# Narrow key and digit loads issued by ScalarE, three in eight high one-hots by ScalarE, and a re-paced copy of x in a graph kernel

## What is computed

```
h = x @ Wn.T + bn;  e = edge_attr @ We.T + be
a = softmax over edges of one dst of leaky_relu(sum((h[src] + e) * attn))
x = layernorm(x + relu(segment_sum(h[src] * a, dst)))
mean = segment_sum(x[dst], src) / max(count, 1)
out = layernorm(x + x @ W1.T + b1 + mean @ W2.T + b2)
```

## Time and profile before

| What | us |
|---|---|
| median of 3 runs (1452.16 to 1456.42) | 1452.87 |
| profiled execution, its own time | 1450.54 |
| its span, first to last instruction | 1448.8 |

### The profile page before, as it was taken

How to read it: one execution, slowest core, us unless ns; L and a number is a source line. 1 busy time by engine, 2 the same in 40 slices (tenths; PEclk the granted TensorE clock), 3 DMA queues, 4 the chain that set the end, 5 groups by cost and what they waited for, 6 DMA issues and landing times.

```text
span 1448.8 us, 26746 instructions
## 1 busy us (share of the span) xinstructions
PE 1247.1 (86%) x7210; PEld 1052.6 (73%) x7210; DVE 1088.4 (75%) x3970; ACT 784.8 (54%) x1768; POOL 749.9 (52%) x731
## 2 busy tenths in 40 slices
PE   4687837992299999589999999999998999999994
PEld 3576726882188888478888888888886888877783
DVE  8588947889655555188888888988888787867761
ACT  5744582560044444257777777777774444544542
POOL 1067763777767777634334103555530555655563
PEclk9999978996599999889999999999999999999997
DMA  6399865998556666556666767898872233223221
GB/s 189 119 277 293 261 180 191 296 313 299 198 82 97 91 100 87 77 187 219 218 226 216 231 216 260 294 298 296 301 243 85 91 98 92 88 90 94 86 79 42
DMA packets 118161, 260.71 MB, mean 180 GB/s; under 512 B 23505, under 2 KB 56872, under 8 KB 118084
## 3 DMA queue, kind: packets, MB, share of 16 engines
q1 hardware_dynamic: 75738, 193.82, 40.9%
q0 software_dynamic: 40128, 64.45, 19.7%
q10 hardware_dynamic: 2218, 1.58, 0.3%
HBM read 182.23 MB, written 130.49 MB: 216 GB/s over the span
## 4 chain that ended last, share of the span: by engine, by line
PE 63%; DMA 10%; POOL 7%; issue 7%; ACT 6%; DVE 5%; SPq 1%; POOLq 0%; ACTq 0%; DVEq 0%
PE bank L1248 35%; PE bank L1238 9%; PE bank L1293 5%; PE bank L1289 5%; PE bank L1245 4%; PE bank L1228 4%; DMA xin<-z_scratch,idx_src 3%; DMA yout<-low_digits_scratch 3%; POOL out_rows L467 3%; ACT aggn L604 3%; POOL xin L464 2%; DMA X<-in_x,idx_src 2%; PE bank L1177 2%; DMA order_scratch<-pay,rank_i 1%; ACT X L609 1%
## 5 line engine op out<-in xcount | busy, mean ns | idle before, releaser
L1248 PE MATMUL bank<-w1T,xT 128*128 128x256 f32 x1968 | 491.4, 380 | 0.0
L1248 PEld LDWEIGHTS bank<-w1T,xT 128*128 128x128 f32 x1968 | 343.7, 191 | 66.5 <-issue 0.3
L473 POOL DMA_INDIRECT order_scratch<-pay,rank_i x200 | 195.0, 975 | 233.6 <-DVE xin L749 106.5
L566 ACT ACTIVATE yout<-bank,nmr,rstd 128x256 f32<-128x256 f32 x492 | 251.7, 577 | 8.1 <-DVE nmr L752 8.0
L557 ACT COPY xT<-bank 128x512 f32<-128x512 f32 x346 | 203.0, 588 | 37.6 <-PE bank L1238 29.0
L916 DVE BATCH_NORM_STATS2 stats<-bank 128x6 f32<-128x512 f32 x246 | 168.5, 694 | 60.7 <-PE bank L1248 60.3
L916 DVE BATCH_NORM_STATS2 stats<-xin 128x6 f32<-128x512 f32 x246 | 158.3, 685 | 73.8 <-DMA xin<-z_scratch,idx_src 52.2
L665 ACT COPY agg<-bank 128x257 f32<-128x257 f32 (+1 forms) x200 | 74.3, 372 | 221.9 <-PE bank L1293 215.1
L512 POOL DMA_INDIRECT z_scratch<-xin,idx_out x100 | 156.4, 1564 | 56.9 <-ACT xin L678 33.8
L749 DVE TENSOR_SCALAR xin<-xin,stats,rstd 128x256 f32<-128x256 f32 x492 | 171.8, 411 | 1.0
L467 POOL DMA_INDIRECT out_rows<-yout,idx_out x100 | 100.0, 1000 | 139.6 <-DMA xin<-z_scratch,idx_src 67.8
(11 more groups left out here) (187 smaller groups left out, 1915.6 us busy)
## 6 DMA issues: line engine op xcount, KB each, us to landing
z_scratch<-in_x SPq DMA_DIRECT2D x125, 400.0 KB
xin<-z_scratch SPq DMA_DIRECT2D x97, 512.0 KB, 4.4
out_rows<-yout SPq DMA_DIRECT2D x97, 512.0 KB, 3.1
yout<-keys_scratch SPq DMA_DIRECT2D x50, 256.0 KB, 6.7
kB<-sorted_scratch SPq DMA_DIRECT2D x50, 256.0 KB, 3.3
yout<-low_digits_scratch SPq DMA_DIRECT2D x50, 128.0 KB, 8.0
xin<-in_edge_attr SPq DMA_DIRECT2D x12, 512.0 KB, 8.8
order_scratch<-pay,rank_i POOLq DMA_INDIRECT x200
```

Source lines behind the costliest of these rows:

```text
L473: g.indirect_dma_start(out=order_dram[k], out_offset=bass.IndirectOffsetOnAxis(ap=rank_i[k][:, t:t + 1], axis=0), in_=pay[:, t, :], in_off ...
L566: a.activation(yout[hu][0:rows, j, :], bank_of(j // 2)[0:rows, (j % 2) * D:(j % 2 + 1) * D], ACT.Identity, bias=nmr[0:rows, slot, j:j + 1] ...
L1248: ins = mm(to, buf[:, jj, c, 0:n], w[:, c, :], start=False, stop=i == len(terms) - 1 and c == 1)
```

## The change

The key scratch becomes 16-bit unsigned and the low-digit scratch 8-bit, so a key spread is 128 KB instead of 256 and a low-digit spread 64 KB instead of 128. VectorE makes the 16-bit copy by one more instruction per sort, ahead of the float copy. The spreads go from SyncE's queue to ScalarE's: three before the DST loop, in the middle of the DST histogram, then the pair of quad n+3 after the odd table copy of quad n. ScalarE makes the high one-hots of tiles 3, 7 and 1 of each eight, VectorE the other five. SyncE sends 20 copies of x beside the DST one-hots, then waits at quad n for VectorE to have used the keys of n quads, and sends one copy at even and two at odd DST quads. The block of 24 copies in the SRC part is unchanged in the text, but stands behind these waits.

```diff
-    keyrow_dram = [nc.dram_tensor(f"keys_scratch{k}", [T, P], F32).ap() for k in (DST, SRC)]
-    lowrow_dram = [nc.dram_tensor(f"low_digits_scratch{k}", [T, P], BF16).ap() for k in (DST, SRC)]
+    keyrow_dram = [nc.dram_tensor(f"keys_scratch{k}", [T, P], U16).ap() for k in (DST, SRC)]
+    lowrow_dram = [nc.dram_tensor(f"low_digits_scratch{k}", [T, P], U8).ap() for k in (DST, SRC)]
...
+        def high_by_act(t):
+            return t % GT == 3 or t % (2 * GT) == 1
...
+            for i in range(10):
+                sp.wait_ge(s_onehot, 2 * i + 1)
+                copy_x(2)
 
             for k in (DST, SRC):
-                sp.wait_ge(s_keyd[k], 32)
                 for q in range(Q):
-                    n = k * Q + q
-                    wait(sp, s_lbT, n - 3)
-                    wait(sp, s_lbA, n - 3)
-                    sp.dma_start(lowB[n % 4], spread(lowrow_dram[k], q)).then_inc(s_lb[n % 4], 16)
-                    wait(sp, s_kbu, n - 3)
-                    sp.dma_start(keyB[n % 4], spread(keyrow_dram[k], q)).then_inc(s_kb[n % 4], 16)
+                    wait(sp, s_kbu, k * Q + q)
                     if k == DST and q % 2 == 1 and q >= 5:
                         load_features((q + 3) // 2)
-                    copy_x(2 if k == DST else 1 if q >= 4 else 0)
+                    copy_x(1 + q % 2 if k == DST else 1 if q >= 4 else 0)
                     if k == SRC and q == 3:
                         for i in range(Q // 2):
                             sp.wait_ge(s_onehot, Q + 2 * i + 1)
                             copy_x(2)
...
-                at = [(GT * q + j, gap_hi[2 * (n % 2) + j // 2]) for j in (1, 3)]
+                at = [(GT * q + j, gap_hi[2 * (n % 2) + j // 2]) for j in range(GT) if high_by_act(GT * q + j)]
...
+            def load_spreads(n):
+                if n >= 2 * Q:
+                    return
+                k, q = n // Q, n % Q
+                if q == 0:
+                    act.wait_ge(s_keyd[k], 32)
+                wait(act, s_lbT, n - 3)
+                wait(act, s_lbA, n - 3)
+                act.dma_start(lowB[n % 4], spread(lowrow_dram[k], q)).then_inc(s_lb[n % 4], 16)
+                wait(act, s_kbu, n - 3)
+                act.dma_start(keyB[n % 4], spread(keyrow_dram[k], q)).then_inc(s_kb[n % 4], 16)
...
+                    if k == DST and q == Q // 2:
+                        for n in range(3):
+                            load_spreads(n)
                     high_onehots(k, q)
...
+                    if i % 2 == 1:
+                        load_spreads(k * Q + i // 2 + 3)
...
+                then(v.tensor_copy(keyrow16[k], keyrow_i[k][:]))
                 v.tensor_copy(keyrow_f[k][:], keyrow_i[k][:]).then_inc(s_keyf, 1)
...
-                    if t % 2 == 0:
+                    if not high_by_act(t):
                         ts(onehot_hi[:, t, :], iota16[:, 0:HC], dig_f[k][:, 1, t:t + 1], None, ALU.is_equal)
```

More of the change, by code:

```diff
@@ L22 @@
 I32 = mybir.dt.int32
+U16 = mybir.dt.uint16
+U8 = mybir.dt.uint8
 DST, SRC = 0, 1
@@ L172, in build @@
         low_i = [t[:].bitcast(I32) for t in (fwd, bwd)]
-        lowrow = [t[:].bitcast(BF16)[:, 0:P] for t in (logit, wrow)]
+        lowrow = [t[:].bitcast(U8)[:, 0:P] for t in (logit, wrow)]
+        keyrow16 = [t[:].bitcast(U16)[:, P:2 * P] for t in (logit, wrow)]
         pair_junk = [junk[:, odd, 0:(odd + 1) * P] for odd in range(2)]
@@ L176, in build @@
         aggn = sb("aggn", [P, GT, D])
-        lowB = [yout[i][:, 2, :].bitcast(BF16) for i in range(4)]
-        keyB = [yout[i][:, 0:2, :].rearrange("p j c -> p (j c)") for i in range(4)]
+        lowB = [yout[i][:, 2, 0:P].bitcast(U8) for i in range(4)]
+        keyB = [yout[i][:, 0, :].bitcast(U16) for i in range(4)]
         spare16 = aggn[:, 2:4, :].rearrange("p j c -> p (j c)").bitcast(BF16)
@@ L586, in _ @@
                 act.wait_ge(s_keyf, 2 * k + 1)
-                act.dma_start(keyrow_dram[k], keyrow_f[k][:]).then_inc(s_keyd[k], 16)
+                act.dma_start(keyrow_dram[k], keyrow16[k]).then_inc(s_keyd[k], 16)
                 act.wait_ge(s_keyf, 2 * k + 2)
```

## The result

The changed kernel takes **1459.08 us** (median of 20 runs, 1453.98 to 1464.07), the kernel before 1454.89 beside it (20 runs, 1449.6 to 1457.53). The ratio is 1.0034, with a 95% interval of 1.0022 to 1.0046: slower by 0.3%, where 1441 and a gain were forecast. The profiled execution's span is 1455.0 us against 1448.8.

The account below looks back on a forecast made before the run. Before 400 us GpSimd was taken to come last, its scatters stalling beside full DMA engines; afterwards TensorE is busy. The terms -3.8 - 14 + 0.8 + 5 = -12.0 gave 1441 us on the median's basis, range 1433 to 1457.

Parts of the forecast that it names:

- part 4: Issues and waits in the tile loops: spreads land within their 6.3 us deadline, no cost; bounds 0 to 25 x 2.8 us.
- part 5: SRC loop: 17 more copies left at its start, the block of 24 at quad 3; +5 us as gathers landing later.
- slower rival: SRC loop: the block saturates DMA, spreads miss their deadline; landing at 8.0 gives 1471, at 9.1 1498; chance 0.12.
- part 3: Behind the order: VectorE's SRC one-hots of tiles 64 to 99 gain four high one-hots, +0.8 us on the path.
- part 2: GpSimd's order scatters: lighter DMA load leaves 3 us of 17 us stall, -14 us; bounds 0 and 17.
- Part 1: ScalarE's DST histogram: 6.8 us saved by fewer one-hots, 3.0 lost to six spread issues, net -3.8 (-4.8 to -2.5).
- no-change rival: DST load: narrow spreads cost as much DMA time as wide, relief about 5 us; net +2, 1455; chance 0.20.

Follow-up runs that it names:

- e1: The changed kernel with the block of 24 copies at SRC quad 0 instead of quad 3: 1443.21 us, ratio 0.9926 to the kernel before.
- e4: The changed kernel with wide spreads again (32-bit keys, 16-bit low digits), still on ScalarE's queue: 1466.31 us, ratio 1.0099 to the kernel before.
- e10: The kernel before with narrow spreads, three-in-eight split and re-paced copies, spreads still on SyncE, block at SRC quad 3: 1451.33 us, ratio 0.9936.
- e11: The changed kernel with the block of 24 copies at SRC quad 0, run once more as a base: 1450.96 us against 1461.22, ratio 0.9937.
- e5: The kernel before with only the three-in-eight split of high one-hots to ScalarE: 1451.38 us against 1457.04, ratio 0.9966.
- e6: The kernel before with only the narrow key and digit scratch, spreads still on SyncE's queue: ratio 1.0006.
- e9: The changed kernel with SRC copies paced two per quad from quad 2 on, no block of 24: 1457.53 us, ratio 1.0001 to the kernel before.
- e12: The kernel before with only eight order scatters in flight instead of six: 1443.44 us against 1452.68, ratio 0.9938.
- e2: The changed kernel with spreads issued after the even table copy, about 2.8 us earlier: 1462.67 us, ratio 1.0059 to the kernel before.

## Why the prediction was wrong

**The step that failed is part 4's landing term.** The prediction bounded a spread's landing between 5.3 us and 9.1, put it "nearest to 5.3", and charged nothing. Measured from 238 to 310 us: 10.4 median, up to 13.9, beyond the upper bound. The bound came from a loop in which SyncE itself paced the copies behind the spreads; here a block of 24 stands in one queue and the spread in another. The same prediction moved that block into this loop (part 5), said in its slower rival that it saturates DMA there, and then priced the spread by a row of a loop that was not saturated. Even that row was the kinder one: it is of keys, while low digits, on which the deadline is set, took 6.2 us in the median and up to 9.1 in the same loop of the kernel before.

The rival had the mechanism and the slack right: it set the point where the gain is gone at a loop loss of 24 us for a gain of 17.0; the loop lost 24.4, and the gain brought to it was 9.0. Its price had every quad late, by 1.7 us or more. Here ScalarE waited in 11 quads, all before 313 us: 33.9 us, less 11 x 0.92 that it idles there anyway, is 23.8. From 312 to 350 us the DMA share is down to 0.83, and the quads are 3.85 us apart again.

In the profiles the miss is 18.2 us (+6.2 for -12.0): the loop and the dot products brought +17.7 where parts 4 and 5 had +5, the scatters gave 7.3 us less than taken, the first scatter came 1.1 us less early, and part 3 and what follows the dot products took 2.8 off. Without the block in the loop (e1) the gain is 10.0 us, near the forecast's 12.0; that is luck in part, since part 2 gave less and part 5's cost is gone there.

The queues from 242 to 282 us suggest how a queue of its own failed to help (packets, MB, share of 16 engines). The changed kernel:

```profile
q1 hardware_dynamic: 2089, 8.96, 61.2%
q0 software_dynamic: 1159, 3.18, 23.2%
q10 hardware_dynamic: 1783, 1.24, 15.5%
```

and e1, with the block gone:

```profile
q0 software_dynamic: 1364, 3.73, 36.8%
q1 hardware_dynamic: 883, 3.78, 25.2%
q10 hardware_dynamic: 2740, 1.87, 23.3%
```

The spreads' queue, q10, moved 0.85 packets for each packet of the copies' queue, q1, and a copy's packet is 4.3 KB (8.96 MB / 2089) and holds an engine for 61.2% x 640 / 2089 = 0.19 us; a spread's is 0.7 KB and holds it 0.06, a gather's 0.13. A quad's two spreads are 7200 / 25 = 288 packets, 18 on each engine. If each of them is followed by one of either other queue, a quad needs 18 x (0.06 + 0.19 + 0.13) = 6.8 us; 40 us x 288 / 1783 = 6.5 were measured, with 1.17 copy packets and 0.65 gather packets for each of a spread. This also fits e4, where wide spreads have as many packets and twice the bytes and landed 1.6 us later. It is a reading of counts, not tried by itself; a spread of fewer packets would try it.

In the Trainium skill (DMA: Bandwidth & Descriptors, "Queues, rings and completion order") each DMA engine goes round its queues by the packet, and a packet there is a group of descriptors. The prediction cited that as protection for a short spread. The counts above agree with equal turns, but they don't tell how many of the trace's packets make one turn. If the turns are equal, a transfer of small packets pays a large foreign one for each of its own, and the rule speaks against the change. The other section of the Trainium skill that the prediction cited, "Issuing engines are not separate DMA queues", agrees with e10 and e11: the ratios are 0.9936 without the move to ScalarE and 0.9937 with it.

**Part 1** came out at -3.8 as forecast, but partly by luck, and its pieces can now be told apart. The issues on ScalarE's queue and the idle time that they cost it, in the changed kernel:

```profile
32.82 0.35 ACTq L648 DMA_DIRECT2D yout<-low_digits_scratch  x1
33.54 0.56 ACTq L650 DMA_DIRECT2D yout<-keys_scratch  x1
...
36.15 1.10 ACTq L650 DMA_DIRECT2D yout<-keys_scratch  x1
37.30 0.81 ACT L607 ACTIVATE aggn<-iota,dig_f 128x196 bf16<-128x196 bf16 x2 [4.02 <-issue]
```

The six issues cost 4.0 us, where 3.0 was taken. Without them e5's histogram, from 20.57 to the first gap of the DST loop at 48.93, is 6.65 us shorter than that of before, where 6.8 was taken. With them the changed kernel's is 2.5 us shorter; the other 1.3 of the 3.8 come from ahead of it, where ScalarE's last weight copy starts at 19.70 us instead of 20.97. Whether the change did that isn't settled.

**Part 2** was mis-sized: 14 taken, 6.7 measured (145.9 to 139.1). On the chip of e6 and e9 it is 10.4 (150.3 to 139.9); e6 stands there for the kernel before. Narrow spreads and fewer copies did lighten the DST loop's load to a share of 0.86, but the prediction made the stalls a matter of load alone and costed no other limit. e12 removes 10 us of them at the full load.

**Part 3** was right in size: the 54 one-hots behind the order became 13 + 13 + 32 = 58, busy for 11.26 us in place of 10.54, and the time from the ordered rows' load to the first gather grew by 0.45.

**Part 5** moved the load where it said, but the +5 was looked for in the gathers. They did land later beside the block, in a median of 7.7 us from 238 to 310 us against 5.9 in the kernel before, but all were there when the dot products came; the spreads paid. The no-change rival fails too: its premise that narrow loads cost as much is against e4's shares. Yet its consequence held for e6, since a lighter load by itself brought nothing there; that six in flight still set the pace in e6 is likely by e12, but e6 was not run with eight.

## What to carry to other kernels

Price a moved transfer in the stage as the change leaves it: if the same edit pushes a block of copies into that stage, the landing must be taken from a stage with that queue in it. A queue of its own did not shield small packets from a deep queue of large ones here, and neither did a lead longer by 2.8 us; keep the deep queue out of that stage, or order copies and small loads in one queue behind the same waits. And where stalls are put down to transfers in flight, try the number in flight first: two more cost one constant here and brought 0.6%.

## What the runs showed of the hardware that was not expected

- The same DMA share of 0.96 went with quite different landings. In e5 the wide spreads in SyncE's queue are issued in turn with one copy per quad. Its stretch from 238 to 310 us, and the landing of its low-digit spreads there:

```profile
238.00:310.00 72.00, 66.59 (x454) 59.92 (x452) 61.21 (x336) 42.69 (x75) 52.87 (x55) 1.00 0.96 300
...
DMA to landing us min/median/max: 5.6/6.6/8.5
```

  In the changed kernel, at the same share, half as wide and on a queue of their own, they landed in 10.4; 36 copies were issued there in this stretch, 19 in e5.
- More lead went with a longer transfer: up to 19.27 us in e2 against 15.75 for the longest of the changed kernel's chain.
- In the changed kernel the six issues back to back on ScalarE's queue took 0.35 to 1.10 us each, and the engine's own next instruction waited for all six.
